# A decoder layer on one core: cross-attention scores and row maxima as pairs of 64-row matmuls, and four tiles of normalised rows written out by indirect DMA

## The reference: what is computed

```python
Q = query @ Wq + bq;  K = key @ Wk + bk;  V = value @ Wv + bv      # 16 heads of d = 8
scores = jnp.einsum('bhqd,bhkd->bhqk', Q, K) / jnp.sqrt(jnp.float32(D_K))
attn = jax.nn.softmax(scores, axis=-1)
out = jnp.einsum('bhqk,bhkd->bhqd', attn, V)
...
for i in range(E):                                                 # E = 8, H = 512
    h = jax.nn.relu(jnp.einsum('bsd,dh->bsh', xi, W1[i]) + b1[i])
    yi = jnp.einsum('bsh,hd->bsd', h, W2[i]) + b2[i]
    out = out + yi * weights[..., i:i + 1]
```

## Time and profile before

| | us |
|---|---|
| median of 3 runs | 326.13 |
| the profiled execution | 326.34 |
| its span, first to last instruction | 324.6 |
| TensorE matmul busy | 297.8 (92%) |
| VectorE busy | 206.5 (64%) |
| ScalarE busy | 193.0 (59%) |
| GpSimd busy | 97.8 (30%) |

### The profile page before, as it was taken

The page is one execution under the profiler, slowest core; times in us unless marked ns, Lnnn a source line. Parts: engine busy times, 40 slices in busy tenths (PEclk is TensorE's granted clock), DMA queues, the critical chain, the costliest instruction groups (busy, mean ns, idle before and its releaser), DMA issues.

```text
span 324.6 us, 5407 instructions
## 1 busy us (share of the span) xinstructions
PE 297.8 (92%) x1869; PEld 210.2 (65%) x1869; DVE 206.5 (64%) x444; ACT 193.0 (59%) x525; POOL 97.8 (30%) x140
## 2 busy tenths in 40 slices
PE   6789999999989899797989788889999999999995
PEld 2578677877777568453745343436778878678883
DVE  3767657375548885966376673536686867666652
ACT  1569858387747664466276668867655465354451
POOL 7990190035020200720056152055558110000000
PEclk9799999999999999999999999979999999999999
DMA  8900015530100010001084491000000000100001
GB/s 234 210 3 3 1 23 65 67 43 16 36 0 2 16 35 2 5 0 45 5 253 141 112 280 55 3 0 2 0 1 2 0 0 0 35 0 0 2 1 32
DMA packets 14889, 14.06 MB, mean 43 GB/s; under 512 B 2620, under 2 KB 10892, under 8 KB 14860
## 3 DMA queue, kind: packets, MB, share of 16 engines
q1 hardware_dynamic: 13278, 12.92, 16.4%
q10 hardware_dynamic: 1584, 0.80, 0.9%
HBM read 9.94 MB, written 0.52 MB: 32 GB/s over the span
## 4 chain that ended last, share of the span: by engine, by line
PE 73%; DVE 13%; ACT 3%; DMA 3%; issue 3%; SPq 2%; POOL 1%; DVEq 0%; ACTq 0%; POOLq 0%
PE ps L663 7%; PE ps L665 7%; PE ps L664 7%; PE ps L737 6%; PE ps L770 5%; PE ps L782 4%; PE ps L944 4%; PE ps L945 4%; PE ps L946 4%; DVE mneg L1306 4%; PE ps L815 3%; PE ps L852 3%; PE ps L744 2%; SPq L412 2%; DMA w_in<-in_L_attn_W_qkv 2%
## 5 line engine op out<-in xcount | busy, mean ns | idle before, releaser
L1062 ACT ACTIVATE p<-ps,negmax 128x256 f32<-128x256 f32 (+1 forms) x128 | 52.7, 426 | 25.2 <-DVE negmax L1277 24.7
L1392 DVE SCALAR_TENSOR_TENSOR hid_lo<-ps,hid_hi 128x512 fp32r<-128x512 f32 x64 | 43.6, 688 | 33.7 <-ACT hid_hi L1126 33.4
L1306 DVE TENSOR_REDUCE mneg<-ps 128x2 f32<-128x512 f32 x64 | 42.5, 684 | 18.6 <-PE ps L815 18.5
L1126 ACT ACTIVATE hid_hi<-ps 128x512 fp32r<-128x512 f32 x64 | 37.5, 598 | 26.8 <-PE ps L665 26.7
L1092 ACT ACTIVATE px<-ps 128x512 f32<-128x512 f32 x64 | 36.1, 598 | 17.8 <-PE ps L837 17.5
L1277 DVE TENSOR_REDUCE negmax<-ps 128x2 f32<-128x512 f32 (+1 forms) x48 | 32.9, 686 | 19.6 <-PE ps L739 12.5
L815 PE MATMUL ps<-k_st,q_mem 128*128 128x256 bf16 x128 | 24.7, 276 | 9.0 <-DVE mneg L1306 7.6
L504 POOL TENSOR_SCALAR tmp<-mv 128x2 f32<-128x2 f32 x8 | 1.9, 233 | 95.3 <-DVE mv L1301 95.3
L1048 ACT CAST t_hi<-ps 128x512 fp32r<-128x512 f32 x32 | 18.8, 592 | 19.5 <-PE ps L665 18.6
L663 PE MATMUL ps<-x_hi,w_hi 128*128 128x512 f32 x64 | 25.6, 400 | 1.7 <-issue 1.5
L1062 ACT ACTIVATION_READ_ACCUMULATOR p<-ps,negmax 128x1 f32 x128 | 26.6, 208 | 0.0
(11 more groups left out here) (184 smaller groups left out, 663.7 us busy)
## 6 DMA issues: line engine op xcount, KB each, us to landing
w_raw<-in_L_ffn_W SPq DMA_DIRECT2D x2, 1024.0 KB, 6.1
w_last<-in_L_ffn_W SPq DMA_DIRECT2D x8, 256.0 KB, 6.1
k_st<-k_part SPq DMA_DIRECT2D x12, 128.0 KB
q_mem<-q_part SPq DMA_DIRECT2D x48, 32.0 KB
w_in<-in_L_attn_W_qkv ACTq DMA_DIRECT2D x2, 384.0 KB, 6.3
w_in<-in_L_attn_W_qkv SPq DMA_DIRECT2D x2, 384.0 KB, 7.1
resid<-in_x SPq DMA_DIRECT2D x2, 256.0 KB, 4.0
p<-in_L_attn_W_o SPq DMA_DIRECT2D x1, 512.0 KB, 8.3
```

Source lines behind the costliest of these rows:

```text
L1062: last = act.activation(dst, bank[:, n * i:n * i + n], ACT.Exp, bias=negmax[:, kt, h:h + 1], accum_out=psums[:, kt, h:h + 1])
L1126: act.activation(hid[0][:, c, :], ps[:, hidden_banks[NC * k + c], :], ACT.Relu).then_inc(s_ha, 1)
L1306: dve.tensor_reduce(mneg[:, qt, :].rearrange("p (r g) -> p r g", r=2)[:, :, g], ps[:, max_bank[("MX", b, u)], :].rearrange("p (h k) -> p h ...
L1392: dve.scalar_tensor_tensor(hid[1][:, c, :], ps[:, hidden_banks[NC * k + c], :], 0.0, hid[0][:, c, :].bitcast(F32), ALU.max, ALU.subtract). ...
```

## The change

1. **Scores.** A slot's two `CS` matmuls of 512 columns over 128 rows become four of 256 columns over 64 rows: the two heads stand in the two halves of the array's rows and in two banks. All four are issued at the first `CS` of the slot, after a wait for both banks. A bank now holds one head with both key tiles, and `px` is laid out to match.
2. **Maxima** of sequences 2 and 3 (PAIRED = 2): units u and u + 1 are issued together, four matmuls of 256 columns over 64 rows, after a wait for both banks. MAXIMA deals them out in pairs, directly behind the scores of the slot.
3. **Banks of the scores:** three in turn also for g < 4 of sequence 3.
4. **GpSimd** writes tiles 0 to 3 of `norm` to a scratch tensor in DRAM with four indirect DMAs by a list of row numbers, behind norm_3(1). SP waits for them at the very end.

```diff
@@ -44,6 +44,7 @@
 LAST_RING = 3
+PAIRED = 2
@@ -173,6 +174,9 @@
         ps = ctx.enter_context(nc.psum_tensor("ps", [P, 8, 512], F32))
+        rows = nc.dram_tensor("rows", [NT * P, D], F32, kind="Internal").ap()
+        row_id = sb("row_id", [P, NT], U32)
+        s_rows = sem("s_rows")
@@ -217,8 +221,8 @@
 
         MAXIMA = (((2, 5), (1, 1, 1, 2, 2, 1, 1), (3, 0), (1, 1, 2, 2, 1), (3, 5)),
                   ((3, 5), (1, 2, 1, 2, 2, 1, 1), (B, 0), (2, 2, 2), (B, 4)),
-                  ((B, 3), (1, 2, 2, 2, 2), (B + 1, 0), (1, 2, 2, 2), (B + 1, 4)),
-                  ((B + 1, 5), (2, 3, 3), (B + 2, 0), (3, 3, 1, 1), (B + 2, 5)))
+                  ((B, 3), (2, 2, 2, 2, 2), (B + 1, 0), (2, 2, 2), (B + 1, 4)),
+                  ((B + 1, 5), (2, 2, 2), (B + 2, 0), (4, 2, 2, 2), (B + 2, 5)))
 
 
 
@@ -280,14 +284,20 @@
 ...
             for g in range(HP):
                 maxima_now, turn = max_plan.get((B + b, g), ([], []))
-                slot = [("CS", b, g, 0)] + tail.get(g - 0.5, []) + more.get((b, g - 0.5), []) + maxima_now[:1] + [("CS", b, g, 1)]
+                paired = maxima_now[:2] if maxima_now and maxima_now[0][1] >= PAIRED else []
+                maxima_now = maxima_now[len(paired):]
+                slot = [("CS", b, g, 0)] + paired + tail.get(g - 0.5, []) + more.get((b, g - 0.5), [])
+                slot += (maxima_now[:1] if not paired else []) + [("CS", b, g, 1)]
                 if b == 0:
                     slot += tail.get(g, [])
                 if g in (2, 4, 6):
                     slot += [("CO", b, g // 2 - 1)]
                 if g == 0 and b >= 1:
                     slot += [("CO", b - 1, 3)]
-                slot += maxima_now[1:2] + turn + (tail.get(g, []) if b else []) + maxima_now[2:] + more.get((b, g), [])
+                if paired:
+                    slot += maxima_now + turn + (tail.get(g, []) if b else []) + more.get((b, g), [])
+                else:
+                    slot += maxima_now[1:2] + turn + (tail.get(g, []) if b else []) + maxima_now[2:] + more.get((b, g), [])
                 if (b, g) < (last, 6):
                     slots.append(slot)
 
@@ -325,7 +335,7 @@
 
         def score_bank(b, k):
 
-            return k % 3 if b < B - 1 else k % 2
+            return k % 3 if b < B - 1 or k < 2 * (HP * (B - 1) + 4) else k % 2
 
         def out_bank(m):
             return 3 + m % 2 if m < 2 * B - 1 else 3
@@ -476,6 +486,7 @@
                     sp.wait_ge(s_misc_ev, misc_at[("YO", hf, i)] + 1)
                     sp.dma_start(out.rearrange(tiles, p=P)[:, ts, :], resid[:, ts, :]).then_inc(s_out, 16)
             sp.wait_ge(s_out, 64)
+            sp.wait_ge(s_rows, 16 * 2 * TPB)
@@ -611,6 +622,13 @@
             norm_3(1)
+
+            step(pool.iota(row_id[:, :], pattern=[[P, NT]], base=0, channel_multiplier=1,
+                           allow_small_or_imprecise_dtypes=True))
+            for t in range(2 * TPB):
+                pool.wait_ge(s_n3, t + 1)
+                pool.indirect_dma_start(rows, bass.IndirectOffsetOnAxis(row_id[:, t:t + 1], 0), norm[:, t, :], None
+                                        ).then_inc(s_rows, 16)
 
             pool.wait_ge(s_xlo, 1)
             first_low(1)
@@ -810,6 +828,20 @@
                         pe.wait_ge(s_vx_ev, 1)
                 if ("MX", b, u) == first_in_5:
                     pe.wait_ge(s_z_ev, 4 * B)
+                if b >= PAIRED:
+
+                    if u % 2 == 0:
+                        for n in range(2):
+                            ge(pe, s_mx_ev, max_before[("MX", b, u + n)])
+                        for i in range(TPB):
+                            for par in range(2):
+                                r = slice(64 * par, 64 * par + 64)
+                                last = pe.matmul(ps[:, max_bank[("MX", b, u + par)], S * i:S * i + S],
+                                                 q_st[b][r, g, S * par + P * i:S * par + P * i + P],
+                                                 k_st[r, g, S * b:S * b + S], start=(i == 0), stop=(i == TPB - 1))
+                                if i == TPB - 1:
+                                    last.then_inc(s_mx, 1)
+                    return
                 ge(pe, s_mx_ev, max_before[("MX", b, u)])
                 for par in range(2):
                     last = pe.matmul(ps[:, max_bank[("MX", b, u)], S * par:S * par + S],
@@ -825,17 +857,24 @@
                                      ident_b[:, :], start=True, stop=True)
                 last.then_inc(s_misc, 1)
 
-            def cross_scores(b, g, kt):
-
-                if g == 0 and kt == 0:
+            def cross_scores(b, g):
+
+                if g == 0:
                     pe.wait_ge(s_mst[b], 16 * 2)
-                k = 2 * (HP * b + g) + kt
-                if k < 3:
-                    pe.wait_ge(s_exp, 12 * B - 2 + k)
-                else:
-                    pe.wait_ge(s_px, last_in(score_banks[k], enumerate(score_banks[:k])) + 1)
-                pe.matmul(ps[:, score_banks[k], :], k_st[:, g, S * b + P * kt:S * b + P * kt + P], q_st[b][:, g, :],
-                          start=True, stop=True).then_inc(s_st, 1)
+                k = 2 * (HP * b + g)
+                for n in (k, k + 1):
+                    if n < 3:
+                        pe.wait_ge(s_exp, 12 * B - 2 + n)
+                    else:
+                        pe.wait_ge(s_px, last_in(score_banks[n], enumerate(score_banks[:n])) + 1)
+                for kt in range(TPB):
+                    for par in range(2):
+                        r = slice(64 * par, 64 * par + 64)
+                        last = pe.matmul(ps[:, score_banks[k + par], S * kt:S * kt + S],
+                                         k_st[r, g, S * b + P * kt:S * b + P * kt + P],
+                                         q_st[b][r, g, S * par:S * par + S], start=(kt == 0), stop=(kt == TPB - 1))
+                        if kt == TPB - 1:
+                            last.then_inc(s_st, 1)
 
             def cross_out(b, g4):
 
@@ -848,7 +887,7 @@
                 for kt in range(2):
                     for j in range(4):
                         h = 2 * g4 + j // 2 + 8 * (j % 2)
-                        p = px[:, g4 % 2, 1024 * (j // 2) + 512 * kt + S * (j % 2):][:, 0:S]
+                        p = px[:, g4 % 2, 1024 * (j // 2) + 512 * (j % 2) + S * kt:][:, 0:S]
                         last = pe.matmul(ps[32 * j:32 * j + 32, out_bank(m), S * (g4 % 2):S * (g4 % 2) + S],
                                          v_pad[:, TPB * b + kt, (DH + 1) * h:(DH + 1) * h + 32], p, start=(kt == 0), stop=(kt == 1))
                 last.then_inc(s_pv, 1)
@@ -973,7 +1012,8 @@
                     elif kind == "mT":
                         max_turn(b)
                     elif kind == "CS":
-                        cross_scores(b, *i)
+                        if i[1] == 0:
+                            cross_scores(b, i[0])
                     elif kind == "CO":
                         cross_out(b, *i)
                     elif kind in ("oq0", "oT0", "oq1", "oT1", "wo"):
@@ -1084,11 +1124,11 @@
                     act.wait_ge(s_misc, misc_at[("PJ", b - 1)] + 1)
                 act.copy(zT[:, 2 * i:2 * i + 2, :], ps[:, ring_bank[("Z", b, i)], :]).then_inc(s_z_ev, 1)
 
-            def cross_probabilities(b, g, kt):
-                k = 2 * (HP * b + g) + kt
+            def cross_probabilities(b, g, par):
+                k = 2 * (HP * b + g) + par
                 act.wait_ge(s_st, k + 1)
                 ge(act, s_pv, 4 * b + g // 2 - 1)
-                c0 = 1024 * (g % 2) + 512 * kt
+                c0 = 1024 * (g % 2) + 512 * par
                 act.activation(px[:, (g // 2) % 2, c0:c0 + 512], ps[:, score_banks[k], :], ACT.Exp,
                                scale=SCALE_X).then_inc(s_px, 1)
 
@@ -1303,7 +1343,8 @@
             def cross_max(b, u):
                 g, qt = u // 2, u % 2
                 dve.wait_ge(s_mx, 16 * b + u + 1)
-                dve.tensor_reduce(mneg[:, qt, :].rearrange("p (r g) -> p r g", r=2)[:, :, g],
+                by_head = mneg[:, :, :].rearrange("p t (r g) -> p t r g", r=2)[:, :, :, g]
+                dve.tensor_reduce(by_head[:, :, qt] if b >= PAIRED else by_head[:, qt, :],
                                   ps[:, max_bank[("MX", b, u)], :].rearrange("p (h k) -> p h k", h=2), AX, ALU.max,
                                   negate=True).then_inc(s_mx_ev, 1)
 
```

## The result

The changed kernel takes 329.58 us (median of 4 runs, 328.72 to 331.01) and the kernel before 326.02 us beside it: ratio 1.0136, 95% interval 1.0083 to 1.0188. It is slower by 1.4%, outside the range of the prediction. The profiled execution took 331.01 us, its span 329.2 us, against 326.34 and 324.6 before.

The account below looks back on a forecast made before the run. From 146 to 214 us it took no engine as the bound, but the handing over between engines. The terms +0.2 + 0.65 - 0.1 - 0.3 + 0.2 gave +0.65 us, so 326.8 us on the median's scale, range 323.6 to 328.3.

Parts of the forecast that it names:

- The halves: Scores and maxima on TensorE: a factor of two from halves side by side; the rival that they do not had 0.08.
- TensorE's saving: TensorE's own work in scores and maxima: 5 us saved, bounds 10.7 saved to 5.8 lost, little of it on the way.
- GpSimd's part: GpSimd's four DMAs: 0 us, hidden in 13.47 us of idle time; the rival that GpSimd is held up had 0.05.
- PJ's start: Sign of being right, ahead of the first fixed point: PJ starts within 0.2 us of 158.5.
- the stacked queries: Sign of being right: a longer wait before the first maxima matmul of sequence 3, which starts at 181.7 to 182.3 us.
- A sign of being wrong: Granted clock over the run: below 1.00 in more than three stretches would speak against the forecast.
- Up to the first fixed point: Up to the landing of sequence 3's stacked queries: +0.2 us, bounds 0 and +0.6, as q comes late.
- To the residual: From 182 us to sequence 1's residual: +0.65 us, bounds -0.4 and +1.5, as VectorE waits behind pairs of maxima.
- The clock: Lower clock as the eight pairs of maxima begin: +0.2 us; one stretch costs 0.2 to 0.5, 0 if none comes.
- the clock stays low: Slower rival, chance 0.13: half clock through most of 181 to 197 us costs 1.5 us more, 328.3 us.
- From the residual to the first expert: Small steps from sequence 1's residual to the first expert's matmul: -0.1 us, bounds 0 and -0.5.
- Behind the first expert: Where TensorE is the bound, with four score matmuls left: -0.3 us, bounds 0 and -0.9.

Follow-up runs that it names:

- E11: E3 plus 3, 4 and 6 matmuls of 512 columns that nobody reads, in three waits TensorE has anyway; 324.01 us, ratio 0.9964 to the kernel before.
- E12: The kernel before plus 3, 3 and 6 matmuls that nobody reads, in three waits TensorE has anyway; 324.40 us, ratio 0.9984.
- E2: The kernel before with only GpSimd's four DMAs, their list of row numbers and the wait for them put in; 325.31 us, ratio 1.0019.
- E10: E1 plus 4, 4 and 6 matmuls of 512 columns that nobody reads, in three waits TensorE has anyway; 329.16 us, ratio 1.0131.
- E3: The changed kernel without GpSimd's part and with the maxima as before, so only the scores as pairs; 324.91 us, ratio 0.9986.
- E4: The changed kernel without GpSimd's part and with the scores as before, so only the maxima as pairs; 328.02 us, ratio 1.0087.
- E1: The changed kernel without GpSimd's four DMAs, their row numbers and the wait for them; scores and maxima both as pairs; 330.78 us, ratio 1.0178.
- E5: E1 with the joint wait of a pair of maxima split, each head waiting for its own bank; 325.90 us, ratio 1.0035.
- E7: E1 with the maxima as before in shape and waits (128 rows, unit by unit), only their places new; 325.91 us, ratio 1.0041.
- E14: E5 plus 3, 4 and 6 matmuls that nobody reads, in three waits TensorE has anyway; 324.78 us, ratio 0.9984.

## Why the prediction was wrong

- **Confirmed.** The halves run side by side. Of TensorE's saving at most some 0.4 us reaches the end (E11 against E12). GpSimd's part is hidden (E2), and a DMA of its costs 0.96 to 1.25 us, within the bounds of 0.66 and 1.28. VectorE stands behind pairs of maxima. PJ's start came about as forecast, though the profiled executions (158.50 and 157.60) can't show it, since the first had a stretch at half clock ahead: at full clock the cheaper scores bring PJ from 157.06 (E12) to 156.54 (E11), and with pairs of maxima, the wait of 0.55 us ahead of it among them, it starts between 157.07 (E10) and 157.71 (E1).
- **Signs that failed.** TensorE waited less and not longer for the stacked queries (0.86 us for 1.13), and `px` waited for CS as long as before. A sign of being wrong came true: there are four stretches at half clock, where more than three were to speak against the forecast.
- **Up to the first fixed point, +0.2 us forecast, +0.75 measured.** PJ to n2T grew by 1.0 us where I had 0.6; q won back 0.3. The round trip of a pair is 0.56 us and not 0.49, which was that of a single unit, and from q on the way is unchanged.
- **To the residual, +0.65 forecast.** At full clock it is 16.40 - 15.14 = +1.26 (E10), inside the bounds of -0.4 and +1.5, but half of it was missing from the sum. The gaps are 0.56 us, and the wait for oq (the one before `r_den`) is 0.71 us where I had 0.1.
- **The clock, +0.2 forecast: the term that failed.** I counted on one stretch at 0.2 to 0.5 us. It was one on the way to the residual (17.68 - 16.40 = +1.3) and two on the way to the first expert (19.69 - 17.39 = +2.3), where I had not looked for any: 3.6 us. A stretch between PJ and the first expert costs 0.7 to 1.5 us, not 0.2 to 0.5, since not only the pairs of maxima get slower but all of TensorE's small steps that others wait for, CO above all (1.94 us for 1.07). The rival "the clock stays low" had the right direction and too small a price, and it looked between 181 and 197 us, where one of the stretches lay; two lay behind, on the way to the first expert, which the prediction had at full clock.
- **From the residual to the first expert, -0.1 forecast.** At full clock the stage is unchanged: 17.39 in E10 as before.
- **Behind the first expert, -0.3 forecast, -0.04 measured.** Both have one stretch at half clock there; without it the stage is 0.6 us shorter in every kernel (109.3 for 109.9), pairs or not. The cheaper scores gain nothing even there.

By runs instead of stages: the kernel before takes 324.05 to 325.1 us at clocks of 0.999 and 1.0, and 325.9 to 326.9 at 0.988 and 0.989, about 2 us for 0.01 of clock. On that line the changed kernel's runs (328.7 and 328.9 at 0.987, 330.2 and 331.0 at 0.979) would be at some 326.3 us at full clock, 2.0 us over the kernel before: the two handing-over terms, 0.75 + 1.26. That is an estimate, for no run of it was at full clock. A second way leads to the same figure: E10's profiled execution took 327.78 us with a single stretch at half clock, which cost 1.5 us, so 326.3 without it. The rest of the loss, 1.6 us between the medians, goes with the clock. So of the 2.8 us by which the forecast of 326.8 missed the median, about half, 1.4, is the clock (1.6 for 0.2), some 1.2 are the two terms of handing over (2.0 for 0.85), and the small gains of 0.1 and 0.3 that did not come make up the rest, all rounded.

**Why the clock fell is not shown.** Three things bear on it.

- In the mean clock, neither part of the change does it alone: it is 0.996 in the kernel before, 0.995 with the scores alone (E3), 0.997 with the maxima alone, their joint wait included (E4), and 0.979 with both (E1). In between lie 0.985 with the wait split (E5) and, with the scores as pairs, 0.991 with only the places of the maxima new (E7). So the low clock comes with both together, and the point that E1 costs beyond E3 and E4 goes with it.
- Ahead of the first low stretch TensorE had many short pauses, the longest between 186 and 193 us one of 1.24 us. The Trainium skill ("TensorE: Matmul & The Clock Gate", A second HAM failure mode: psum-queue depth-cycling) tells of a kernel in which TensorE idles briefly and often between groups of matmuls and the clock goes up and down; that much the trace agrees with.
- But the pauses don't decide it. In E10 TensorE has the same instructions there and the same pauses (again 1.24 us at most), it was busy even less, and its clock stayed full:

```profile
191.00:194.00 3.00, 1.38 (x14) 0.68 (x12) 2.44 (x5) 1.94 (x4) 2.56 (x4) 1.00 1.05 307
194.00:197.40 3.40, 2.98 (x34) 1.55 (x34) 2.61 (x10) 1.51 (x5) 0.00 (x0) 1.00 0.67 199
```

And ahead of the low stretch at 206.8 us TensorE had been busy for 2.67 of 3.40 us. What decides in a given run is left open.

## What to carry to other kernels

Ask of a cheaper matmul first what it must wait for. Two units that were handed over one by one kept both engines busy; joined to a pair with a common wait they left VectorE idle for a round trip most times, and splitting that wait gave most of it back with the scores as pairs (4.7 of 5.9 us) and about half with the scores as before. Look at the granted clock of every stretch before and after a change: here two changes that each left the mean clock alone lowered it together, and a stretch at half clock cost 0.7 to 1.5 us even where TensorE wasn't the bound, because others wait for its small steps. Work in a wait that exists anyway cost nothing here, and the clock was full in most runs with it (9 of 10 in E12, but only 5 of 10 in E14); the same work on the way cost as much as it gave back.

## What was not expected of the hardware

A stretch at half clock cost 1.0 to 1.3 us in the cross-attention, where TensorE is not the bound, and 0.6 us at the start of the experts, where it nearly is. The same kernel differs by 2 us from run to run with the clock (324.3 us at 1.0, 326.5 at 0.989), more than the limit of 0.98 us that the prediction set for a change to be told.
